# Rotating k on GpSimd between the loops, and two orders inside a decoder layer's scan loop

## The reference

```
x = x + mamba(ln(x))              # in-projection to 2 x 1024, causal conv of 4 taps, silu,
                                  # selective scan over 16 states, gate, out-projection
x = x + cross_attention(ln(x), ctx)   # 32 heads, 8 k/v heads, D = 128
x = x + experts(ln(x))            # 64 experts of rank 8, top 16 by a router
```

```
q = (x @ Wq);  k = (ctx @ Wk);  v = (ctx @ Wv)
cos, sin = cos_t[position_ids], sin_t[position_ids]
q = q * cos + rotate_half(q) * sin        # rotate_half(x) = concat(-x2, x1)
k = k * cos + rotate_half(k) * sin
attn = softmax(where(mask == 0, -1e9, q @ k.T / sqrt(D)))
out = (attn @ v) @ Wo
```

## Time and profile before

| what | value |
|---|---|
| time, median of 3 runs | 2400.57 us (2399.07 to 2403.79) |
| profiled execution, first to last instruction | 2396.3 us |
| PE / DVE / ACT / POOL busy | 88% / 75% / 44% / 25% |
| the three loops of mamba and attention, each | 350 to 351 us |
| iteration 0 up to its last scan chunk | 354.7 us |
| last iteration, attention alone | 371 us |

### The profile page before, as it was taken

How to read it: one execution, slowest core, us unless ns; L and a number is a source line. 1 busy time by engine, 2 the same in 40 slices (tenths; PEclk the granted TensorE clock), 3 DMA queues, 4 the chain that set the end, 5 groups by cost and what they waited for, 6 DMA issues and landing times.

```text
span 2396.3 us, 27137 instructions
## 1 busy us (share of the span) xinstructions
PE 2107.1 (88%) x8244; PEld 1194.4 (50%) x8248; DVE 1786.4 (75%) x1801; ACT 1059.8 (44%) x2613; POOL 588.9 (25%) x405
## 2 busy tenths in 40 slices
PE   6877888989999979989999979989999987799987
PEld 2332453445555534445555534445555533577763
DVE  3499994389999975289999985279999984355533
ACT  2544441465565522365665522365655521243330
POOL 0099981001111120001111110001111120566530
PEclk9888999899999989899999989889999999799888
DMA  1468893148888771238888871238888772122210
GB/s 62 166 152 198 213 213 121 54 133 187 181 177 187 166 173 53 72 123 179 176 189 179 181 172 60 72 106 172 176 196 175 171 173 82 65 90 97 88 44 18
DMA packets 110074, 328.98 MB, mean 137 GB/s; under 512 B 12945, under 2 KB 13073, under 8 KB 107569
## 3 DMA queue, kind: packets, MB, share of 16 engines
q0 software_dynamic: 35328, 127.94, 28.7%
q1 hardware_dynamic: 68912, 189.58, 26.3%
q10 hardware_dynamic: 5760, 10.49, 1.2%
HBM read 183.00 MB, written 14.94 MB: 83 GB/s over the span
## 4 chain that ended last, share of the span: by engine, by line
DVE 40%; PE 31%; issue 18%; DMA 5%; ACT 3%; DVEq 1%; POOL 1%; SPq 1%; POOLq 0%; ACTq 0%; PEldq 0%
DVE hs L1130 13%; PE acc L1443 5%; DVE hs L1137 5%; DVE hs L1300 5%; PE pq L1488 4%; DMA xc<-hs 3%; DVE hs L1121 3%; DVE qr L1167 2%; PE pq L1732 2%; PE pq L1496 2%; PE pq L1526 2%; PE acc L1655 2%; PE pk L1732 2%; PE acc L1565 2%; DVE sc L1187 1%
## 5 line engine op out<-in xcount | busy, mean ns | idle before, releaser
L706 POOL DMA_DIRECT2D xc<-hs x192 | 165.8, 866 | 1301.6 <-DVE hs L1137 1263.9
L1130 DVE TENSOR_TENSOR_SCAN hs<-dA,hs 128x1024 f32<-128x1024 f32 x192 | 428.9, 2276 | 0.0
L888 ACT ACTIVATE dA<-dt,aneg 128x504 f32<-128x504 f32 x384 | 253.5, 707 | 250.9 <-DVE hs L1130 250.7
L1496 PE MATMUL pq<-qT,wa 128*128 128x512 f32 x768 | 354.8, 616 | 9.2 <-DVE sc L1187 9.2
L1576 PE MATMUL acc<-wb,oT 128*128 128x512 f32 x768 | 351.7, 602 | 3.6 <-ACT oT L876 3.6
L1137 DVE TENSOR_TENSOR hs<-hs,bc 128x1024 f32<-128x1024 f32 x256 | 307.9, 1205 | 2.2
L853 ACT ACTIVATE pr<-sc,mx 128x64 f32<-128x64 f32 x512 | 170.8, 335 | 247.4 <-DVE mx L1193 247.4
L1443 PE MATMUL acc<-xnT,wa 128*128 128x512 f32 x512 | 232.2, 607 | 11.5 <-PE acc L1443 4.4
L1496 PEld LDWEIGHTS pq<-qT,wa 128*128 128x128 f32 x768 | 146.9, 197 | 183.8 <-issue 173.7
L1121 DVE TENSOR_TENSOR hs<-u,bc 128x1024 f32<-128x1024 f32 x192 | 226.3, 1219 | 8.2 <-ACT xc L976 5.9
L1526 PE MATMUL pq<-kT,qp 128*128 128x64 f32 x1024 | 190.9, 289 | 41.2 <-DVE kT L1146 16.3
(11 more groups left out here) (200 smaller groups left out, 3312.7 us busy)
## 6 DMA issues: line engine op xcount, KB each, us to landing
xc<-hs POOLq DMA_DIRECT2D x240, 512.0 KB, 6.9
bc<-bc_rows SPq DMA_DIRECT2D x64, 512.0 KB, 7.5
wa<-in_wq SPq DMA_DIRECT2D x64, 512.0 KB, 10.2
wb<-in_wo SPq DMA_DIRECT2D x64, 512.0 KB, 5.8
wa<-in_wx SPq DMA_DIRECT2D x16, 512.0 KB, 4.2
wa<-in_wz SPq DMA_DIRECT2D x16, 512.0 KB, 4.9
wb<-in_ow SPq DMA_DIRECT2D x16, 512.0 KB, 7.2
k<-k_rows SPq DMA_DIRECT2D x32, 256.0 KB, 11.1
```

The lines of the kernel that those rows point to most:

```text
L888: ins = S.activation(to[:, :, 1:SEQ], dt[:, s, :].rearrange("p (b t) -> p b t", t=SEQ)[:, :, 1:SEQ], ACT.Exp, scale=aneg[:, s, bass.ds(jj ...
L1130: V.tensor_tensor_scan(out=hs[:, c, :], data0=dA[:, c % 2, :], data1=hs[:, c, :], initial=0.0, op0=ALU.mult, op1=ALU.add).then_inc(scd.sem, 1)
L1496: ins = M.matmul(pq[:, h, :], wa4(p)[:, k, h * P:(h + 1) * P], qT[:, k, :], start=(k == 0), stop=(k == KE - 1))
```

## The change

The k of blocks 0 to 2 are no longer rotated by DVE inside the loop. POOL does it between the loops, for the whole block at once: four passes (`turn_k`), each of which loads two head groups and their swapped halves from DRAM, rotates them with three instructions of 128x1024, and stores them to a new DRAM tensor (`k_turned_rows`). In the loop SP then loads rotated k straight into `kT` and `k2T`; the k of the next group is loaded when the scores that read the present one are done. The k of block 3 (iteration 4) is still rotated by DVE.

The rotary tables of all blocks are gathered at the start, turned on PE and stored to DRAM as eight more early units of iteration 0, and loaded per block behind the loop. The load of x for block 0's second use moves into the loop of iteration 0, since the gathered rows stand in its buffer until then.

In the loop, DVE inverts the softmax sums right behind the third scan chunk instead of behind the fourth and a product, and ACT scales the probabilities ahead of its copy of o.

```diff
@@ SP, in the loop's step
-                            if p == 0:
-                                eng.wait_ge(krdy.sem, krdy.upto(blk, 0) + jj)
+                            if p == 0 and mamba:
+                                eng.wait_ge(sd.sem, sd.upto(blk, 1) + jj * 2)
                                 hold(eng)
-                                load_k(blk, jj + 1)
+                                load_turned_k(blk, jj + 1)
...
@@ SP, iteration 0
+                        if n == NBLK:
+                            eng.wait_ge(s_eun, first_unit[NBLK])
+                            eng.dma_start(xr[:, :, :], a["x"][0]).then_inc(s_xr, 16)
...
@@ SP, behind the loop
+                    load_tables(i)
...
-                    eng.wait_ge(krdy.sem, krdy.upto(i, -1))
-                    hold(eng)
-                    load_k(i, 0)
+                    if not nxt:
+                        load_raw_k(i, 0)
...
+                if nxt:
+
+                    eng.wait_ge(s_kst, i * (8 * KVH) + 8 * KVH)
+                    hold(eng)
+                    load_turned_k(i, 0)
                 if attn:
                     eng.wait_ge(outr.sem, outr.upto(blk, 0))
                     eng.dma_start(out[blk], xn).then_inc(s_out, 16)
@@ POOL, behind the loop
+                    rstd(i, ln2, ln2r, TT)
+
+                def turn_k(m):
...
+                    if m:
+                        eng.wait_ge(s_kst, i * (8 * KVH) + 16 * m)
+                        hold(eng)
+                    G.dma_start(raw, kscr[i, 2 * m:2 * m + 2].rearrange("g p t -> p g t")).then_inc(s_kraw, 16)
+                    for h in range(2):
+                        G.dma_start(swp[h * 64:(h + 1) * 64, :, :],
+                                    kscr[i, 2 * m:2 * m + 2, (1 - h) * 64:(2 - h) * 64, :].rearrange(
+                                        "g p t -> p g t")).then_inc(s_kraw, 16)
+                    two = [P, 2, T]
+                    eng.wait_ge(s_kraw, i * (24 * KVH) + 48 * (m + 1))
+                    hold(eng)
+                    G.tensor_tensor(raw, raw, cosT[:, :].unsqueeze(1).to_broadcast(two), ALU.mult).then_inc(kc1.sem, 1)
+                    G.tensor_tensor(swp[:, :, :], swp[:, :, :], sinT[:, :].unsqueeze(1).to_broadcast(two),
+                                    ALU.mult).then_inc(kc2.sem, 1)
...
+                    G.tensor_tensor(raw, raw, swp[:, :, :], ALU.subtract).then_inc(kcd.sem, 1)
...
+                    G.dma_start(turned[i, 2 * m:2 * m + 2].rearrange("g p t -> p g t"), raw).then_inc(s_kst, 16)
...
+                    eng.wait_ge(s_cs, i * 32 + 32)
                     hold(eng)
-                    for t in range(TT):
-                        eng.indirect_dma_start(
...
+                    for m in range(KVH // 2):
+                        turn_k(m)
@@ ACT, the loop's step
-                    if attn and mamba and p == 1 and not tail:
-                        turn_k(jj + 1)
...
                     if mamba and not last:
                         decay(jj, p + 1, 0)
+                    if mamba and attn and not last:
+                        normalise(jj, p + 1)
                     if attn:
                         evac_o(jj, p)
                     if mamba and not last:
                         decay(jj, p + 1, 1)
...
-                    if mamba and attn and not last:
-                        normalise(jj, p + 1)
@@ DVE, the loop's step
                         scan(i, jj, p, 2)
-                        scan(i, jj, p, 3)
-                    if mamba:
-                        times_c(i, jj, p, 2)
-                    if soft:
+                    if soft and mamba:
                         invert_sum(jj, p + 1)
                     if mamba:
+                        scan(i, jj, p, 3)
+                        times_c(i, jj, p, 2)
                         times_c(i, jj, p, 3)
...
                         rope_q(jj, p + 2)
-                        if p == 0:
+                        if not mamba and p == 0:
                             rope_k(jj + 1)
@@ PE, scores
-                        eng.wait_ge(krdy.sem, krdy.upto(blk, o // 2) + jj)
-                        eng.wait_ge(k2r.sem, k2r.upto(blk, o // 2) + jj)
+                        eng.wait_ge(s_k1, blk * (16 * KVH) + (o // 2 + 1) * 16 + jj * 16)
+                        eng.wait_ge(s_kr, blk * (32 * KVH) + (o // 2 + 1) * 32 + jj * 32)
```

More of the change, by code:

```diff
@@ L356, in build @@
         outr = stage("out_ready", 1)
-        ch_p = stage("dve_positions", 2)
+        s_chp = sem("dve_positions")
         ch_a = stage("dve_mixture", 2 + 8 * TT)
@@ L589, in one @@
                 if mamba:
-                    eng.wait_ge(pid.sem, pid.upto(i, -1))
-                    hold(eng)
-                    eng.dma_start(posi[:, :], a["pos"][i]).then_inc(s_pos, 16)
+                    if attn:
+                        eng.wait_ge(q1r.sem, q1r.upto(blk, PAIRS - 1))
+                        hold(eng)
+                        eng.wait_ge(q2r.sem, q2r.upto(blk, PAIRS - 1))
+                        hold(eng)
+                    else:
+                        for n in range(2):
+                            eng.wait_ge(s_est[n], 16 * (first_unit[NS] // 2))
+                    load_tables(i)
                     if not attn:
@@ L660, in _ @@
             rstd(0, ln1, ln1r, TT)
+            eng.wait_ge(s_pid, 1)
+            for b in range(NBLK):
+                for t in range(TT):
+                    eng.indirect_dma_start(
+                        out=tab(b, t), out_offset=None, in_=a["rotary"],
+                        in_offset=bass.IndirectOffsetOnAxis(ap=posu[:, b * TT + t:b * TT + t + 1], axis=0)).then_inc(
+                            s_tab, 16)
             def one(i, mamba, attn, nxt):
@@ new lines, in one @@
+                if nxt:
+                    if attn:
+                        eng.wait_ge(sd.sem, sd.upto(i - 1, PAIRS - 1))
+                    else:
+                        for n in range(2):
+                            eng.wait_ge(s_est[n], 16 * (first_unit[NS] // 2))
+                        eng.wait_ge(scd.sem, scd.upto(0, NS * NCH - 1))
+                    eng.wait_ge(s_cs, i * 32 + 32)
+                    hold(eng)
+                    for m in range(KVH // 2):
+                        turn_k(m)
@@ L981, in one, with read_unit @@
                         S.activation(silu_z(s), acc[:, s % 4, :], ACT.Silu).then_inc(szr.sem, 1)
-                def read_unit(at, what):
+                def read_unit(at, what, b, g):
+                    scale = float(D) ** -0.5 if what == "k" else -1.0 if what == "table" and g == 1 else 1.0
                     eng.wait_ge(s_eun, at + 1)
@@ L1228, in one @@
                     eng.wait_ge(s_mask, blk * 32 + 32)
[L1229 to L1230 removed]
+                    eng.wait_ge(s_cs, blk * 32 + 32)
+                    if not mamba:
+                        rope_k(0)
                     rope_q(0, 0)
@@ L1675, in early_unit @@
                     ctx_t = early_ctx[b % 2]
+                    if what == "table":
+                        eng.wait_ge(s_tab, 16 * TT * NBLK)
+                        for t in range(TT):
+                            ins = M.transpose(acc[:, 2 + at % 2, t * P:(t + 1) * P], tab(b, t)[:, g * D:(g + 1) * D],
+                                              ident[:, :])
+                        ins.then_inc(s_eun, 1)
+                        return
                     eng.wait_ge(s_ectx[b % 2], 16 * (b // 2 + 1))
```

141 lines of the change are left out of this document (74 added, 67 removed).

## The result

The change made the kernel **slower**: 2462.05 us (median of four, 2455.50 to 2477.57) against 2399.82 us (2398.57 to 2403.79), a ratio of 1.0265 with the 95% interval [1.0227, 1.0304]. That is 62 us, where 20 were forecast. Both profiled executions of it stand in the table. The parts are cut at the first scan and at the end of the last scan of each loop, read from DVE's timeline.

The account below looks back on a forecast made before the run. DVE was taken to bound the loop, with PE close behind, and PE's waits the stretch behind it. Terms -8 - 4 + 30 + 0 + 2 = +20 us gave a median of 2420 us, range 2406 to 2440.

Parts of the forecast that it names:

- The rotation leaves DVE: In the loop: DVE saves 2.0 us once in a pair of steps, at most 42 us in all.
- The scaling ahead of the copy of o: In the loop: o is out 11.3 us after the masking instead of 9.3, so the next masking waits 1.1 us.
- The forecast pair of 44.3 us: In the loop: two steps take 42.7 us without the rotation plus 1.6 us from the late copy of o.
- The term of -8: The loops' net gain: 0.4 us in each of 21 pairs, bounds 0 and -42.
- Rotated k loaded in the loop: In the loop: loading rotated k costs nothing, with 2 to 3 us of cover left.
- SP loses three issues: Behind the loop: out-projection weights go out and land earlier, -2 us in each of two gaps, -4 in all.
- POOL's passes: Between loops: four passes of 17.0 us delay q's weights in the first gap, +30 us, bounds +23 and +70.
- Second and third gap: Later gaps between loops: q's weights still land in time, cost 0 up to passes of some 18.5 us.
- Iteration 0: First loop: table units fit beside the scans, gathers lie under the in-projection, loading x there costs +2 us.
- The rival with long passes: Between loops: POOL's passes take 22 us, first gap pays 50 us, others 10 each, 2460 us; chance 0.15.
- That the loops could give back their 42 us: In the loops: copies of o don't hold PE up, pairs fall to 42.7 us, 2387 us; chance 0.08.

Follow-up runs that it names:

- e1: Changed kernel with ACT's copy of o put back ahead of the scaling, sums still inverted early: 2422.38 us, ratio 1.0104.
- e2: Kernel before with only the early inverse and the scaling ahead of the copy of o, DVE still rotating k: 2445.39 us, ratio 1.0202.
- e6: Changed kernel with copy of o first, POOL's passes in B and C's buffer, first weights ahead of tables, rotary gathers late: 2365.69 us.
- e9: The kernel of e6 run once more, against the kernel before: 2369.99 us, ratio 0.9883.

## Why the prediction was wrong

The direction and the two places were right, the size was not: +20 forecast, +62 measured, outside the range.

- **The rotation leaves DVE**: right. The step without v takes 21.47 us, 21.33 was forecast; with the copy of o first (e1) it is 21.34, and the loops fall by 31.6 us.
- **The scaling ahead of the copy of o**: this is the step that failed first. The mechanism was as described: the copy leaves late, PE waits for it before v, DVE for the scores. The forecast pair of 44.3 us is in the trace too, 21.47 + 22.91 = 44.4 in the quickest pairs. But "The pair takes 42.7 + 1.6 = 44.3 us" took PE's wait as always the same, and its clock as always at the higher level, though the sum itself let PE wait in every pair. In the runs the wait goes up to 3.3 us in pairs where DVE waits for the sums of y first, and behind 9 of 21 waits v runs 5.46 us in place of 3.83; such steps take up to 25.9 us. The term of -8 came out at +16.4, and +12.7 in the second profile. The 24 us between are these two, by an estimate from the rows: 9 slow projections at 1.6 us make 15, and 17 waits of DVE for the sums of y, which the sum put at nothing, make 10. e1 and e2 show that the late copy of o and the slow projections of v come from this order and from nothing else of the change; the waits for the sums of y stay in e1.
- **Rotated k loaded in the loop**: right at nothing. PE nowhere waits for it. Its landing is 3.4 us in the median of all 24 loads, and 4.5 and 5.0 in the first two loops, far from the 11.1 that I took.
- **SP loses three issues**: right in direction. PE's wait for the weights fell from 4.17 to 3.07 us in the second gap and from 3.69 to 3.35 in the third. From the last scan to POOL's last root it is 40.5 and 42.2 us there, where it was 45.3 and 44.0: 6.7 us, 4 were forecast. But 2.8 of them are the granted clock behind that wait in the second gap (0.72 in the mean of the next 10 us before, 1.00 now), and 1.5 an earlier start of PE in the third.
- **POOL's passes**: the mechanism was right, the term too small. Its instructions took 2.35 us, as taken. The three loads took 6.8 us for 5.9 and the turn from product to store and back some 1 us more: 18.7 us a pass for 17.0. From the first load at 417.00 to SP's load of k at 492.09 four passes took 75.1 us, not 68. PE's wait was 31.75 us for 28, and the lower clock behind it cost 9.99 - 7.03 = 3.0 us at the product of q, where 2 were put down; from there to the first scan it is 62.3 us in both kernels. With 4.5 us from SP's other wait, below, that is 39 of the gap's +43 for +30. The other 4 lie ahead of PE's long wait: behind a wait of 3.18 us that every kernel here has, `x_proj` and the transposes ahead of it ran at the lower clock, `x_proj` in 9.42 us for 7.08. Both profiles of the changed kernel have this, but in e6 and e9, which are one kernel, it took 9.45 and 7.08 us; that the change brings these 4 us is not shown.
- **Second and third gap**: wrong. They would cost nothing "up to passes of some 18.5 us". One of four passes took 24.0 and 24.9 us there, mostly because the store's landing held POOL for 7.67 and 7.42 us instead of 3.2, and PE waited 2.74 and 7.29 us for the weights of q. With the gain on SP and the lower clock behind the waits, +3.7 and +8.3 are left.
- **Iteration 0**: mis-sized, +9.8 for +2. The gathers don't lie under the in-projection for nothing: e6 moves them, and the wait of 3.6 us goes, of which 2.7 us are left at the last scan. The loop itself takes some 4 us longer in every kernel with the change (230.9 to 233.8 us; 227.5 and 228.5 without it). Whether the eight table units, their stores or the load of x do that wasn't tried.
- **Missed altogether**: SP's wait for ACT's early stores stands ahead of the first out-projection weights, 4.5 us on the path. The order of SP's instructions had moved there too, and I had priced only the issues that left.

The rival with long passes gave 2460 us, which is near the result, but for another reason: passes of 22 us in all gaps are not what the trace shows. That the loops could give back their 42 us was put at 0.08 and needed the copy of o in time; e1 shows that one swap does it, for 32 of the 42.

What the Trainium skill's page SBUF — State Buffer (section Who interferes with whom) has on the port that POOL and DVE share, which stood behind that rival, made no difference in the gaps: POOL's instructions of 128x1024 took 2.33 to 2.36 us in all twelve passes. More than half of DVE's work beside them (17 of 32 us) was the conv, one of whose inputs is in PSUM. The Trainium skill's page DMA: Bandwidth & Descriptors (section Anatomy of one DMA) gave 3.2 us for the store, and the median landing of the stores was 3.2. For the last load it gave 2.6 us, which with the 2.7 put down for the issues makes an estimate of 5.3; the loads, three in a row, took 6.8 us to the last landing.

## What to carry to other kernels

Before work is handed to an idle engine, look at who has to wait for its end and what is queued behind that waiter: here 75 us of POOL's work cost some 40 us only because the weights of q stood behind it in SP's queue, and nothing that the gaps show once the waiter had its own place. When two engines are both nearly full, an instruction put ahead of another on a third engine is priced by who reads the second one's result, and a wait of some 2.5 us on TensorE cost up to 1.6 us more in the product behind it. A change of several parts is worth taking apart: the two edits that undo the losses were worth 40 us each, and what is left of the change then gains about 30.

## What the runs showed of the hardware

In the loops of the changed kernel PE is busy 91% of the time. Ahead of v it waited 1.8 to 3.3 us; behind 9 of these 21 waits TensorE's granted clock was at its lower level, and 32 products that take 3.83 us took up to 5.47. The length of the wait does not tell which level follows: waits of 2.19 and 2.27 us were followed by the higher and the lower level (e2), and the same wait of 3.18 us ahead of the first `x_proj` by the lower in e6 and the higher in e9, two executions of one kernel. Behind waits of up to 1.55 us (e1) no projection of v was slowed, but behind waits of 1.47 us (e2) halves of o's projection were, nine times. The `x_proj` of e6, then of e9:

```profile
444.20 9.45 PE L1699 MATMUL acc<-xc,xpw 128*64 128x512 f32 x16 [0.77 <-ACT qT L894]
```

```profile
441.50 7.08 PE L1699 MATMUL acc<-xc,xpw 128*64 128x512 f32 x16 [0.93 <-ACT qT L894]
```

The landing of the same kind of DMA differs from place to place far more than I allowed: k of 256 KB landed in 11.1 us when SP loaded it in the busy part of a step, and in 3.4 us in the median of the changed kernel's loads behind the scores and between the loops. What makes the difference no run separates. The DMA issues of the changed kernel:

```profile
k_turned_rows<-qp POOLq DMA_DIRECT2D x12, 512.0 KB, 3.2
kT<-k_turned_rows SPq DMA_DIRECT2D x24, 256.0 KB, 3.4
```

POOL's store of 512 KB held the next pass for some 3.2 us, and in one pass of four of the later gaps for over 7.
